# Smaller projection pieces in the attention slots, shared gates from split parts, and a last softmax division that stays on chip

## The reference

```python
xn = (x - mean) / sqrt(var + 1e-5)                 # over the last axis
q, k, v = Wq @ xn + bq, Wk @ c + bk, Wv @ c + bv   # 16 heads of 16 channels
x = x + Wo @ (v softmax(q.T k / 4)) + bo
ln = (x - mean) / sqrt(var + 1e-5)
h = ln * rsqrt(mean(ln ** 2) + 1e-6) * w           # 2048 tokens of width 512
shared = (silu(h @ sg) * (h @ su)) @ sd            # hidden width 256
routed = top 2 of 8 experts, each silu(h @ g) * (h @ u) @ d, weighted
x = x + shared + routed
```

## Time and profile before

| what | us |
|---|---|
| runs shown | 850.09, 851.98, 853.51 (median 851.98) |
| the profiled execution's own time | 849.69 |
| its span | 847.9 |
| PE busy in the span | 803.9 (95%) |
| DVE busy | 518.1 (61%) |
| ACT busy | 401.1 (47%) |
| POOL busy | 353.1 (42%) |

### The profile page before, as it was taken

One profiled execution on the slowest core, in us unless ns is written; L12 is line 12 of the kernel. 1 busy time (PEld: TensorE's weight loads), 2 busy tenths in 40 slices (PEclk: granted clock), 3 DMA queues, 4 the chain that ended last, 5 costly groups with the idle time before them and its releaser, 6 DMA issues. The chain is left out here.

```text
span 847.9 us, 11463 instructions
## 1 busy us (share of the span) xinstructions
PE 803.9 (95%) x3771; PEld 388.6 (46%) x3771; DVE 518.1 (61%) x1043; ACT 401.1 (47%) x751; POOL 353.1 (42%) x288
## 2 busy tenths in 40 slices
PE   6999999999999999999999998999999999999993
PEld 2434434444444444444433454443555555555552
DVE  5787888787777877878788655568542222222221
ACT  1115666767677677676776663110422323333231
POOL 4207417326354274253220211000117777777774
PEclk9999999999999999999999999999999999999998
DMA  8957557646665566466633223931626555655553
GB/s 275 211 95 224 114 127 166 132 103 141 145 137 129 119 157 149 103 149 143 131 80 106 91 77 110 415 111 51 251 56 99 98 97 97 101 90 96 95 98 43
DMA packets 54956, 110.48 MB, mean 130 GB/s; under 512 B 12580, under 2 KB 27684, under 8 KB 50660
## 3 DMA queue, kind: packets, MB, share of 16 engines
q1 hardware_dynamic: 37852, 80.23, 37.5%
q0 software_dynamic: 16960, 29.37, 18.4%
q10 hardware_dynamic: 88, 0.16, 0.1%
HBM read 68.44 MB, written 41.16 MB: 129 GB/s over the span
## 5 line engine op out<-in xcount | busy, mean ns | idle before, releaser
L963 DVE TENSOR_REDUCE negmax<-front_ps 128x1 f32<-128x512 f32 x512 | 323.6, 681 | 85.9 <-PE front_ps L816 85.5
L725 ACT ACTIVATE probs<-st_ps 128x512 f32<-128x512 f32 x512 | 280.2, 601 | 166.6 <-PE st_ps L850 149.9
L1215 POOL DMA_INDIRECT out<-x_sb,row_i x78 | 122.0, 1564 | 70.3 <-ACT x_sb L1263 57.0
L1408 PE MATMUL big_ps<-w_gu,attn 128*128 x312 | 140.4, 593 | 0.8 <-ACT attn L1255 0.8
L1602 DVE TENSOR_TENSOR zeros<-attn,big_ps 128x256 f32<-128x256 f32 x39 | 16.4, 421 | 116.3 <-ACT attn L1275 116.3
L850 PE MATMUL st_ps<-stacks 50*128 50x512 f32 x256 | 77.7, 488 | 5.4 <-ACT probs L725 4.3
L1408 PEld LDWEIGHTS big_ps<-w_gu,attn 128*128 128x128 f32 x312 | 56.2, 190 | 57.0 <-issue 57.0
L410 POOL TENSOR_TENSOR attn<-attn,recip 128x512 f32<-128x512 f32 x15 | 19.2, 1278 | 150.1 <-DMA recip<-rec_dram 150.1
L850 PE MATMUL st_ps<-q_stack,k_stack 50*128 50x512 f32 x256 | 74.6, 491 | 3.9 <-ACT probs L725 2.8
L580 POOL CAST early<-early 128x512 fp32r<-128x512 f32 x28 | 17.1, 610 | 136.4 <-ACT early L678 136.4
L816 PE MATMUL front_ps<-stacks 48*128 48x512 f32 x256 | 68.7, 434 | 3.8 <-DVE negmax L963 3.0
(11 more groups left out here) (199 smaller groups left out, 1056.6 us busy)
## 6 DMA issues: line engine op xcount, KB each, us to landing
parts_dram<-early SPq DMA_DIRECT2D x32, 512.0 KB, 6.2
stacks<-parts_dram SPq DMA_DIRECT2D x32, 256.0 KB, 5.6
w_gu<-in_gate_up SPq DMA_DIRECT2D x8, 1024.0 KB, 13.4
x_sb<-in_x SPq DMA_DIRECT2D x8, 512.0 KB, 9.9
early<-in_ctx POOLq DMA_DIRECT2D x8, 512.0 KB, 7.1
stacks<-parts_dram SPq DMA_DIRECT2D x32, 128.0 KB, 5.9
k_stack<-parts_dram SPq DMA_DIRECT2D x16, 256.0 KB, 5.1
q_stack<-parts_dram SPq DMA_DIRECT2D x16, 256.0 KB, 5.6
```

What stands on the lines that cost most here:

```text
L725: nc.scalar.activation(probs[:, k % 2, u % GH, :], score_bank(UNITS * s + u), ACT.Exp, scale=SCALE).then_inc(exp_done, 1)
L963: nc.vector.tensor_reduce(negmax[:, n % 2, c:c + 1], smax_bank(UNITS * n + u), AX_X, ALU.max, negate=True).then_inc(max_done, 1)
L1215: nc.gpsimd.indirect_dma_start(outs[i], bass.IndirectOffsetOnAxis(ap=row_i[:, k:k + 1], axis=0), y_sb[:, k % RING, DY * i:DY * (i + 1)], N ...
L1408: mm = nc.tensor.matmul(gu_ps[:, :], h_t[:, k % 2, a, :], w_gu[:, bass.ds(expert, 1), a, :], start=(a == 0), stop=(a == DT - 1))
```

## The change

In slots 3 to 12 every piece is cut in half, and the halves stand at units 2, 6, 10 and 14 (K, then Q) and 18, 22, 26 and 30 (V or output). The turn of the maxima goes to unit 8, with its copy in the same unit of DVE's order. ACT's or DVE's emptying of a piece follows two units after its second half, for the last piece at unit 0 of the next slot. The waits and the order of SP and POOL follow. The attention's high part gets a home of its own, in the places of `zeros` and `rms_bc`, and is split per half; the loads of `rms_bc` and the router's weights move to slot 13, and `zeros` is cleared again there for slot 14.

The two reciprocal roots become one, from the variance scaled by 1 + 1e-6. The shared gates become three fp32r products of parts: POOL splits their weights in slot 14, ACT writes the high part of `h` and DVE the low part, the first group in slot 15, the other three in the middle stage. The last numerators and denominators are picked out by four matmuls with pieces of the identity (`last_half`) in place of the way through DRAM, and the middle stage is put in another order. Of `w_gu` the first expert and of `down` all are loaded later. The row constants of rows 12 and 13 are found in slot 15, and four more rows of `h` are stored ahead of the barrier.

```diff
-        KQ_UNITS = (2, 6)
         FIRST_UNITS = (2, 4, 8, 10)
+        FIRST_ROWS = (6, 10, 14, 22)
         AHEAD = 4
 
+        def spread(s):
+
+            return 3 <= s < HALVES - 3
+
         def turn_unit(s):
 
-            return 16 if s == 0 else 12
+            return 16 if s == 0 else 8 if spread(s) else 12
+
+        def parts_unit(s):
+
+            return turn_unit(s) if spread(s) else turn_unit(s) + 2
+
+        def kq_units(s):
+
+            return ((2, 6), (10, 14)) if spread(s) else ((2, 2), (6, 6))
 
         def late_units(s):
 
...
+        def rows_high(act, g, pieces):
+
+            act.wait_ge(h_stored[g], 16 * GT)
+            act.wait_ge(h_turned, GT * (g + 1))
+            act.wait_ge(ht_ready, GT * (g + 1))
+            nc.scalar.activation(ht_high[:, g, pieces, :], ht_all[:, g, pieces, :], ACT.Copy).then_inc(ht_high_ready, 1)
+
+        def rows_low(dve, g, pieces, ready):
+
+            dve.wait_ge(ht_high_ready, ready)
+            dve.wait_ge(lg_ready, GT * (g + 1))
+            nc.vector.tensor_tensor(ht_low[:, g, pieces, :], ht_all[:, g, pieces, :], ht_high[:, g, pieces, :].bitcast(F32),
...
-                        load_stack(s + 3, 0)
-                        write_part(s + 3, 1)
+                        if not spread(s):
+                            load_stack(s + 3, 0)
+                            write_part(s + 3, 1)
                     if s + 1 < HALVES:
                         rows_out(s + 1)
+                    if proj and spread(s):
+                        load_stack(s + 3, 0)
                     if s > 0:
                         rec_out(sp, s - 1)
                     if s + 1 < HALVES:
                         rows_in(s + 1)
+                    if proj and spread(s):
+                        write_part(s + 3, 1)
                     if s > 0:
                         rec_in(sp, s - 1)
                     if proj:
                         load_stack(s + 3, 1)
                     if s == HALVES - 3:
...
                         sp.wait_ge(v_ready, 2 * B)
                         sp.dma_start(sh_gu[:, :, :], sh_gate_up).then_inc(shared_loaded, 16)
...
                     pool.wait_ge(attn_ready, ATTN_START + 2 * (b + 1))
-                    pool.wait_ge(low_ready, 2 * min(2 * b + 7, HALVES))
-                    nc.gpsimd.tensor_copy(attn_high[:, :, :], attn[:, b % 2, :, :]).then_inc(attn_high_ready, 1)
-                    pool.wait_ge(attn_high_ready, b + 1)
-                    nc.gpsimd.tensor_tensor(attn_low[:, b % 2, :, :], attn[:, b % 2, :, :], attn_high[:, :, :].bitcast(F32),
-                                            ALU.subtract).then_inc(attn_split, 1)
+                    if b == 0:
+                        pool.wait_ge(dump_cleared, 16 * (1 + YCUT))
+                        pool.wait_ge(nm_parts_ready, turns(3))
+                    else:
+                        pool.wait_ge(y_ready, CT * b)
+                    for kt in range(CT):
+                        half = attn[:, b % 2, kt, :]
+                        nc.gpsimd.tensor_copy(attn_high[kt][:, :], half).then_inc(attn_high_ready, 1)
+                        pool.wait_ge(attn_high_ready, CT * b + kt + 1)
+                        nc.gpsimd.tensor_tensor(attn_low[:, b % 2, kt, :], half, attn_high[kt][:, :].bitcast(F32),
+                                                ALU.subtract).then_inc(attn_split, 1)
...
+                        nc.gpsimd.memset(zeros[:, :], 0.0).then_inc(zeros_ready, 1)
+                    if s == HALVES - 2:
+                        pool.wait_ge(shared_loaded, 16 * 2)
+                        for a in range(DT):
+                            nc.gpsimd.tensor_copy(sh_gu_high[:, a, :], sh_gu[:, a, :]).then_inc(sh_high_ready, 1)
+                            pool.wait_ge(sh_high_ready, a + 1)
+                            nc.gpsimd.tensor_tensor(sh_gu_low[:, a, :], sh_gu[:, a, :], sh_gu_high[:, a, :].bitcast(F32),
+                                                    ALU.subtract).then_inc(sh_split, 1)
                     if s == HALVES - 1:
-                        for t in range(STORED):
+                        for t in range(2 * GT):
                             store_h(pool, t)
                     if s > 0:
                         divide(pool, s - 1)
+                    if s == HALVES - 1:
+                        for t in range(2 * GT, STORED):
+                            store_h(pool, t)
...
-                        if proj and u - 2 in KQ_UNITS:
-                            qk_bias(s + 3, KQ_UNITS.index(u - 2))
-                        if value_batch(s) is not None and u - 2 in late_units(s):
-                            v_copy(value_batch(s), late_units(s).index(u - 2))
+                        if u == 0 and spread(s - 1) and value_batch(s - 1) is not None:
+                            v_copy(value_batch(s - 1), 1)
+                        if proj and ended_at(kq_units(s), u) is not None:
...
                         pe.wait_ge(xn_ready, n // 2 + 1)
+                        if spread(s):
+                            pe.wait_ge(nm_parts_ready, turns(s + 1))
...
 
                 def turn_max(n):
-                    pe.wait_ge(qk32_ready, 2 * min(n + 3, HALVES))
...
-                        if s + 3 < HALVES and u in KQ_UNITS:
-                            project_qk(s + 3, KQ_UNITS.index(u))
+                        i, kts = halves_at(kq_units(s), u)
+                        if s + 3 < HALVES and kts:
+                            project_qk(s + 3, i, kts)
                         if u == turn_unit(s) and s + 1 < HALVES:
                             turn_max(s + 1)
-                        if value_batch(s) is not None and u in late_units(s):
-                            project_v(value_batch(s), late_units(s).index(u))
-                        if out_batch(s) is not None and u in late_units(s):
-                            for kt in range(CT):
-                                project_out(pe, out_batch(s), late_units(s).index(u), kt, proj_ps[:, :])
+                        i, parts_here = halves_at(late_units(s), u)
+                        if value_batch(s) is not None and parts_here:
+                            project_v(value_batch(s), i, parts_here)
+                        if out_batch(s) is not None:
...
+                            for kt in parts_here:
+                                project_out(pe, out_batch(s), i, kt, proj_ps[:, :])
...
                             invert(dve, s - 1)
-                        if u == turn_unit(s) + 2 and s + 1 < HALVES:
+                        if u == 0 and spread(s - 1) and out_batch(s - 1) is not None:
+                            residual(dve, out_batch(s - 1), 1, proj_ps[:, :])
+                            row_stats_of(out_batch(s - 1), 1)
+                        if u == parts_unit(s) and s + 1 < HALVES:
                             max_parts(s + 2, UNITS)
-                        if out_batch(s) is not None and u - 2 in late_units(s):
-                            residual(dve, out_batch(s), late_units(s).index(u - 2), proj_ps[:, :])
-                        if out_batch(s) is not None and u - 4 in late_units(s):
-                            row_stats_of(out_batch(s), late_units(s).index(u - 4))
...
-                numerators_out(sp, HALVES - 1)
-                den_in(sp, HALVES - 1)
-                num_in(sp, HALVES - 1)
-                rec_out(sp, HALVES - 1)
-                rec_in(sp, HALVES - 1)
-                for e in range(E):
+                for e in range(1, E):
                     sp.dma_start(w_gu[:, e, :, :], gate_up[e]).then_inc(wgu_loaded, 16)
-                sp.wait_ge(h_stored, 16 * NTILE)
-                sp.wait_ge(h_turned, NTILE)
-                for e in range(KEPT):
-                    sp.dma_start(w_dn[:, e, :, :], down[e]).then_inc(wdn_loaded[e], 16)
...
                 sp.wait_ge(found_ready, 1)
+                for e in range(KEPT):
+                    sp.dma_start(w_dn[:, e, :, :], down[e]).then_inc(wdn_loaded[e], 16)
+                sp.wait_ge(shgu_ready, FT * GROUPS)
                 for e in range(KEPT, E):
                     sp.dma_start(w_dn[:, e, :, :], down[e]).then_inc(wdn_loaded[e], 16)
+                sp.dma_start(w_gu[:, 0, :, :], gate_up[0]).then_inc(wgu_loaded, 16)
...
                 def shared_gates(j, which=(0, 1)):
                     g, c = j // FT, j % FT
-                    pe.wait_ge(ht_ready, GT * (g + 1))
+                    if j == 0:
+                        pe.wait_ge(sh_split, DT)
+                    pe.wait_ge(ht_split, DT + g)
                     if j >= 2:
                         pe.wait_ge(shact_ready, j - 1)
                     for i in which:
+                        cols = slice(i * F + c * P, i * F + (c + 1) * P)
                         for a in range(DT):
-                            mm = nc.tensor.matmul(big_ps[:, 2 * (j % 2) + i, :], sh_gu[:, a, i * F + c * P:i * F + (c + 1) * P],
```

(50 more changed lines are left out.)

255 lines of the change are left out of this document (159 added, 96 removed).

## The result

The changed kernel takes 838.41 us (median, 831.79 to 841.2) where the kernel before takes 851.94 beside it; the ratio is 0.9845, with a 95% interval of 0.9816 to 0.9874. That is faster, inside the range (816 to 842) and 10 us above the 828 that I forecast: of 24 us of gain, 13.5 came. The profiled execution took 836.97, its span is 835.0.

A forecast was written before the change was run, and what follows sets the result against it. TensorE was taken to bound the attention slots and middle stage, apart from some waits. 849.7 - 14 (slots 3 to 12) - 0.5 (slots 13 to 15) - 10 (middle stage) = 825, 827.5 against the median; forecast 828 us, range 816 to 842.

The forecast's parts named there:

- The step of 3.21 us: Attention slots 3 to 12: with a half piece in each, every step takes 3.21 us, replacing alternating 3.91 and 2.94.
- The residual's waits, 0.6 a slot: Attention slots: PE newly waits for DVE's residual and the maxima delayed behind it, losing 0.6 us per slot.
- The turned maxima, 0.2: Attention slots, units 8 to 10: Q's first half waits 0.2 us for the copy of the turned maxima.
- The bounds of the slots: Slots 3 to 12: expected 14 us less; 20 if no new wait appears, 7 if each slot waits twice as long.
- Slots 13 to 15, -0.5: Last slots before the barrier: the single root saves 1 us in slot 14, extra slot 15 work costs 0.5.
- Gate steps, 5.55: Middle stage: twenty-four fp32r products take 5.55 us a gate step; eight steps 44.4 in place of 55.0, -10.6.
- Rival E: Shared gates: in runs of 24, products come 0.215 us apart, saving another 3 us, total 825; chance 6%.
- The one-hots, a wait of 2: Middle stage: PE waits 0.5 to 3 us, taken as 2, for DVE's one-hots, in place of an earlier 1.81.
- The late loads, "nothing": Before the routed blocks: late w_gu and two down expert loads cost nothing, covered by eight down products, 14 us.
- the bound of -4: Middle stage: smallest expected gain, 4 us instead of 10, if the splits of h fall on DVE's way.
- Rivals A, B and C: A: attention gives nothing, 848, 6%; B: middle stage gives nothing, 837.5, 12%; C: second stack late, slower, 863, 3%.
- Rival D: Attention and middle stage: the new waits for the residual and the one-hots vanish, total 818.5; chance 14%.

The follow-up runs named there:

- e1: The changed kernel with the halves undone, every piece whole again and the residual and statistics placed as before the change; 845.05 us.
- f3: The changed kernel with the shared gates as one plain fp32 product per weight tile in place of three fp32r products; 845.0 us.
- e2: The changed kernel with DVE's residual at the unit of the output piece's second half and the statistics two units later; 830.74 us.
- g0_same: The changed kernel once more, word for word, to see the spread of times and clocks; 836.94 us.
- f1: On e2, six early down loads go ahead of two row stores and the last w_gu load ahead of two down loads; median 4.0 us lower.
- f2: On e2, the sixteen logits products stand one or two at a time behind the twelve large products of gate step 2's first half; 827.96 us.
- g1: On e2, with f1, f2 and f4, two filler products ahead of the barrier and slot 3's root of the rows earlier; 824.85 us.
- g3: On g1, half of gate step 7 goes ahead of the one-hot products and three down loads behind the stores of rows 6 and 7; 825.89 us.
- f4: On e2, the turned maxima are copied between two maxima and K is emptied one exponential earlier; turn's step 3.62 us in place of 3.79, slot 26.35.

## Why the prediction was right, and where not

Faster was right, and so were the two mechanisms that carry the gain: e1 takes back the slots' part, f3 most of the gates'. The profiled execution was to fall by 24.5 us and fell by 12.7. Of the signs that I named, the steps and the gate steps came; slots 3 to 12 (265 to 271) took 272.6, the middle stage to the first block (90 to 93) 94.9, and the late start of the blocks for `w_gu`, which I had called a sign of being wrong, came too. Step by step:

- **The step of 3.21 us.** Measured 3.22, in all spread slots; the stall of two pairs in a row is gone. The 0.7 us a slot for more switches between row-split and full products is in those 3.22, as the half's own first distance of 0.33 is the earlier trace rows.
- **The residual's waits, 0.6 a slot.** Measured 0.45 + 0.2 in odd slots and 0.73 in even ones. Right in place and size. What I did not ask is whether it had to be: e2 takes it away with a change of place.
- **The turned maxima, 0.2.** Measured 0.36 (3.79 less 3.22 less 0.21). Of the 0.37 between 26.7 and 27.07 a slot, 3.3 us over nine slots, this mis-sized term is 0.16, the residual's waits are 0.09, and the rest is one or two hundredths in each step.
- **Slot 3, 1 us more than the others.** Measured 1.8.
- **The bounds of the slots.** 9 x 25.9 + 27 is 260.1, so the bound without a new wait is 21.8 us less and not 20. And the steps with a piece come to PE's own sum within 0.01 us only in the two that I looked at; slot 7 has them up to 4.05 (285.12 to 289.17).
- **Slots 13 to 15, -0.5.** Measured +1.1, of which the stretch at 450.9 is 0.4; g0_same, without it, has +0.7. This step failed: I took 1 us off the wait for the turned maxima in slot 14, and it is 1.0 in g0_same where it was 0.8. What I did not see is that the statistics, now in one burst with the residual, hold up the maxima of slots 13 and 14 (1.5 us of waits), for in e2, where they come later, the stage takes 85.6 us. Why the shorter root gave nothing stays open.
- **Gate steps, 5.55.** Measured 5.58 to 5.61, the products 0.231 apart. Rival E (0.215) is out. The ratio to plain fp32 is 0.81 or 0.82, that of the rows. The four passes of the Trainium skill's page "FP8 and Floating Point Precision", section "TensorE Precision Notes", would give three quarters; the measurement decides.
- **The last half, 2.0.** Measured 1.95 at the full clock, so two do run side by side; 3.65 in the profile of the changed kernel. The reciprocal takes 3.36 and is hidden, as said.
- **The one-hots, a wait of 2.** Measured 2.5. The waits ahead of the transposes and of the last output product were 2.2 and 0.9 in the profile of before; 0.4 is left, so they gave 2.7 where I had counted 1.1.
- **The late loads, "nothing".** This step failed. I counted the issues and 14 us of cover. The transfer took 14.75 us, for `w_gu` shared the DMA engines with eight loads of 512 KB; and these were late since SP's queue held them behind two stores that wait for PE's next products. In f1, with six of them 9 us ahead and two behind, it took 6.0. PE waited 1.9 us.
- **The clock, which no step spoke of.** The earlier trace rows say 1.00 and I carried that over. This is the largest single error: the changed kernel's runs have 0.987 where those of before have 0.995, and the four stretches in the profile cost 4.9 us. Where the middle stage lost it, one difference in order is that four sets of transposes and four of logits now stand close together, which stood in twos between long products before. The denser gates are not needed for it (f3), and with the logits mixed among large products no profile lost it there (f2, g1, g3), but two of four with the logits in a run on the same kernel did not either, so the cause is not shown. The Trainium skill, "TensorE: Matmul & The Clock Gate", section "Why this matters for your kernels", warns of idle gaps between bursts of matmuls. Here the clock fell some 2.9 us into a run of 3.87 us in which PE issued sixteen products of eight columns without a gap. What brings the stretches there, at slot 3's end, at slot 14's start and at the barrier stays open; they come in some executions of a kernel and not in others.

By stage, the spans were to fall by 24.5 and fell by 12.95. The 11.55 between them are 4.75 of the attention, 1.6 of slots 13 to 15, 4.7 of the middle stage and 0.5 before and behind. In the middle stage the clock alone is 4.5; the 1.1 more for `w_gu` (1.9, less the 0.8 for ACT that stood there before) and the 0.5 at the one-hots are made up for by the 1.6 more from the waits ahead of the transposes. So at the full clock it would have come to -9.8, next to my -10, by errors that cancel. That the total lies in the range is in part luck: the bound of -4 there was meant for splits of `h` in DVE's way, and the clock, which is what took the stage down to -5.3, had no term.

Rivals A, B and C are out: the attention gave 9.25, the middle stage 5.3 in spite of three stretches, and PE has no wait for a stack in slots 3 to 12. Rival D was half of the way open: e2 shows that the residual's waits could be had, f4 half of the turned maxima's.

## What to carry to other kernels

Where work is moved into a fixed order by hand, check for each consumer not only whether it has time but where in its own order the new piece stands: 5 us lay in a residual that stood two units too late in DVE's queue, and a wait of 1.9 in loads that stood behind two stores in SP's. When a stage gets faster, look for what its slowness had covered; here a third of the products' gain came back as waits one stage on. And a time worked out at the granted clock of before holds only if the clock stays: read it for every execution ahead of comparing two, and where it fell, compare the same piece of the program with and without. Whether products of few columns bring the fall when they stand in a run is worth a test of its own; here it is a lead, not a finding.
